# Self attention of a transformer decoder layer on one core: merged narrow blocks, batches of units, and tables that place every maximum singly

## The reference

```python
q, k, v = heads(yn @ wq.T + bq), heads(yn @ wk.T + bk), heads(yn @ wv.T + bv)
scores = einsum('bhqd,bhkd->bhqk', q, k) / sqrt(32) + rel_bias + causal   # 2048 x 2048 for each head
attn = softmax(scores, axis=-1)
y = y + merge(einsum('bhqk,bhkd->bhqd', attn, v)) @ w_out.T + b_out
```

## Time and profile before

| what | value |
|---|---|
| median of 3 runs | 2791.2 us (2790.24 to 2792.56) |
| the profiled execution | 2795.43 us, span 2793.4 us, mean granted clock 0.987 |
| TensorE matmul busy | 2702.4 us, 97% |
| VectorE busy | 1583.1 us, 57% |
| ScalarE busy | 1262.0 us, 45% |
| self attention | 396.8 to 1598.7 us |

### The profile page before, as it was taken

One profiled execution on the slowest core, in us unless ns is written; L12 is line 12 of the kernel. 1 busy time (PEld: TensorE's weight loads), 2 busy tenths in 40 slices (PEclk: granted clock), 3 DMA queues, 4 the chain that ended last, 5 costly groups with the idle time before them and its releaser, 6 DMA issues. The chain is left out here.

```text
span 2793.4 us, 40069 instructions
## 1 busy us (share of the span) xinstructions
PE 2702.4 (97%) x12704; PEld 1791.0 (64%) x12704; DVE 1583.1 (57%) x3827; ACT 1262.0 (45%) x2656; POOL 417.2 (15%) x497
## 2 busy tenths in 40 slices
PE   7999989999999999999999899999999999999998
PEld 6788854444444444444444378767778888888886
DVE  5554367777777777777777377567643222222211
ACT  2322113555555555555555545588833322332231
POOL 5000021000000000000000332188556000000000
PEclk9999988999999999999999999999999999999999
DMA  7656663222222222222222398555431000000000
GB/s 223 214 194 200 197 163 83 69 67 69 69 69 70 70 71 69 61 63 60 56 58 54 90 243 259 197 176 182 149 114 50 16 31 31 30 0 30 31 16 15
DMA packets 138950, 272.96 MB, mean 98 GB/s; under 512 B 24886, under 2 KB 56118, under 8 KB 133499
## 3 DMA queue, kind: packets, MB, share of 16 engines
q1 hardware_dynamic: 133530, 255.14, 31.7%
q0 software_dynamic: 5216, 15.33, 1.8%
HBM read 176.02 MB, written 99.98 MB: 99 GB/s over the span
## 5 line engine op out<-in xcount | busy, mean ns | idle before, releaser
L1302 ACT ACTIVATE sa_pr<-sa_st 128x512 f32<-128x512 f32 (+3 forms) x1280 | 611.0, 532 | 536.8 <-DVE sa_st L1365 293.8
L1268 PE MATMUL sa_ov<-sa_pr,sa_v 128*33 128x512 f32 (+3 forms) x2560 | 535.0, 539 | 0.0
L1349 DVE TENSOR_REDUCE sa_part<-sa_mp 128x1 f32<-128x512 f32 x760 | 408.3, 583 | 115.1 <-PE sa_mp L1247 114.3
L1257 PE MATMUL sa_st<-sa_q,sa_k 97*128 97x512 f32 (+3 forms) x1280 | 441.4, 413 | 17.9 <-ACT sa_pr L1302 13.5
L1257 PEld LDWEIGHTS sa_st<-sa_q,sa_k 97*128 97x128 f32 x1280 | 216.3, 189 | 319.7 <-ACT sa_pr L1302 213.0
L1247 PE MATMUL sa_mp<-sa_k,sa_q 96*128 96x512 f32 (+1 forms) x1256 | 362.0, 382 | 10.3 <-PEq L1229 5.3
L1346 DVE CUSTOM_DVE_ANT_0 sa_mp<-sa_mp,sa_ub 128x512 f32<-128x512 f32 (+1 forms) x496 | 308.4, 665 | 77.0 <-PE sa_mp L1247 72.9
L149 PE MATMUL ff_f<-sa_q,ff_w 128*128 128x512 f32 x1024 | 337.2, 390 | 3.1 <-PEq L2068 3.1
L2063 PE MATMUL ff_o<-ff_w,ca_q 128*128 128x512 f32 x1280 | 330.0, 392 | 3.7 <-DVE ca_q L2114 3.7
L2114 DVE TENSOR_TENSOR ca_q<-ca_v,ca_q 128x512 fp32r<-128x512 f32 x128 | 97.5, 762 | 379.3 <-ACT ca_q L2098 379.3
L1268 PEld LDWEIGHTS sa_ov<-sa_pr,sa_v 128*33 128x33 f32 x2560 | 122.0, 110 | 256.2 <-issue 206.6
(11 more groups left out here) (240 smaller groups left out, 3276.7 us busy)
## 6 DMA issues: line engine op xcount, KB each, us to landing
sa_q<-scratch_q SPq DMA_DIRECT2D x96, 256.0 KB, 7.7
sa_k<-scratch_k SPq DMA_DIRECT2D x96, 256.0 KB, 8.9
scratch_q<-sao_qst SPq DMA_DIRECT2D x32, 512.0 KB, 6.6
ca_q<-scratch_q SPq DMA_DIRECT2D x32, 512.0 KB, 4.6
...
sa_v<-scratch_v SPq DMA_DIRECT2D x16, 528.0 KB, 13.0
scratch_o<-sa_osb SPq DMA_DIRECT2D x128, 66.0 KB
```

The lines of the kernel that those rows point to most:

```text
L1257: pe.matmul(st[bank(u, h)][:, 0:w], ks[n.par][:, h, kb * P:(kb + 1) * P], qs[n.par][:, h, g * GW + c0:(g + 1) * GW], start=True, stop=True ...
L1268: last = pe.matmul(ov[64 * h:64 * h + VW, c0:GW], vs[n.par][:, kb, h, :], pr[:, u % 4, h, 0:GW - c0], start=(u in opens), stop=(u in ends))
L1302: act.activation(pr[:, u % 4, h, 0:w], st[bank(u, h)][:, 0:w], ACT.Exp, scale=SCALE).then_inc(s["exp"], 1)
L1349: dve.tensor_reduce(to, tile, AX_X, ALU.max).then_inc(s["red"], 1)
```

## The change

- **Blocks.** A unit may now hold two narrow blocks. Letters name the kinds: F a far block, B the one before the diagonal, D the first diagonal block (512 wide), P the blocks of 384 and 128 columns side by side in one tile for each head, J the block of 256 columns with both heads in one tile. A slot has 36 units and 68 tiles in place of 40 and 80. A tile has one wait for its bank, one exponential, and one bias addition if it has a bias.
- **Batches.** Rounds of two units become batches of two, the last of each group of three: 16 a slot. In batch j TensorE issues the tiles of batch j + 1 with maxima between them, then the values of batch j.
- **Maxima.** Products for one head are placed singly: `MAX_BEFORE[j][i]` says how many go ahead of the i-th tile, the last entry how many follow. A second table, `REDUCED_BEFORE`, gives the order on VectorE. Four single PSUM banks take the place of two double ones. Work for the next slot begins at batch 6, and the turn of group 2 (product 54 of 84) falls into the last batch of the slot before, that of group 3 (83) into batch 5.
- **Opening.** Seven products go before the first score tile, and the first slot has tables of its own.
- **SyncE.** In every slot but the first the queue is now `load(n + 1)`, `row(n, 2)`, `store(n, 0)`, `row(n, 3)`, `row(n + 1, 0)`, `row(n + 1, 1)`, `store(n, 1)`, `store(n, 2)`, `store(n, 3)`. Ahead of the first slot only `row(0, 1)` stands. The table `sa_tb` has 128 more columns, by a DMA of its own.
- **Rooms.** `sa_pr` has six slots for units in place of four; sums and inverses lie in an existing tile.

```diff
-SELF_ORDER = ((0, 2, 3, 1),
-              (2, 4, 1, 6, 0, 3, 7, 5),
-              (6, 10, 3, 7, 4, 11, 1, 8, 0, 9, 2, 5),
-              (5, 12, 15, 0, 1, 3, 2, 13, 8, 14, 10, 11, 7, 9, 6, 4))
-STEPS_FROM = 12
-STEPS_PER_UNIT = (2, 2, 1, 0, 2, 0, 1, 0, 2, 1, 1, 1, 2, 0, 2, 1, 1, 0, 2, 1,
-                  1, 2, 1, 1, 2, 1, 2, 0, 1, 1, 1, 2, 1, 0, 1, 1, 1, 2, 0, 1)
-INVERSE_AT = 4
-OPENING_STEPS = 16
-OPENING_PER_UNIT = (3,) * 8 + (2, 2, 0, 0)
+SELF_ORDER = ('DPJ', 'FPFDFBJ', 'FPFFBJFFFFD', 'FPFFFFJDFBFFFFF')
+BATCHES = ((3,), (2, 2, 3), (2, 2, 2, 2, 3), (2, 2, 2, 2, 2, 2, 3))
+SLOTS = 6
+MAX_FROM = 6
+OPENING_MAX = 32
+MAX_BEFORE = ((1, 2, 0, 1, 0), (2, 3, 0, 0, 1), (1, 1, 3, 0, 0, 1), (4, 0, 1, 1, 0), (0, 1, 3, 0, 0), (0, 0, 1, 0),
+              (2, 2, 0, 1, 3), (0, 1, 0, 1, 1, 2, 4), (1, 2, 0, 1, 1), (1, 1, 0, 1, 3), (3, 0, 1, 3, 1),
+              (0, 1, 3, 0), (0, 0, 2, 0, 0), (2, 0, 2, 1, 0), (0, 0, 2, 1, 1, 1, 0), (0, 0, 1, 3, 1, 0))
+REDUCED_BEFORE = ((4, 0, 0), (6, 0, 0), (3, 3, 0, 0), (3, 1, 2), (4,), (1, 0, 0, 0), (8,), (5, 2, 2), (4, 0, 1),
+                  (6,), (8,), (2, 0, 0, 2), (1, 1, 0), (5,), (5,), (0, 0, 1, 2, 0, 2))
+OPENING_MAX_BEFORE = ((2, 5, 0, 2, 1), (5, 0, 2, 0, 0), (3, 1, 0, 2, 3, 0), (3, 2, 0, 0, 4), (3, 1, 0, 2, 1),
+                      (2, 2, 0, 2), (0, 2, 0, 0, 5), (2, 1, 2, 0, 1, 0, 0), (1, 1, 1, 3, 1), (0, 2, 2, 0, 1),
+                      (1, 2, 0, 2, 1), (0, 1, 3, 0), (2, 1, 2, 0, 1), (0, 4, 1, 0, 1), (2, 3, 0, 1, 1, 1, 0),
+                      (0, 0, 3, 0, 1, 2))
+OPENING_REDUCED_BEFORE = ((8, 2, 0), (6, 1, 0), (8, 0, 1, 0), (6, 0, 3), (7,), (3, 1, 0, 2), (7,), (6, 0, 0),
+                          (5, 0, 2), (5,), (6,), (0, 3, 0, 1), (5, 1, 0), (6,), (8,), (0, 0, 2, 0, 0, 4))
+INVERSE_AT = 1
+
+
+Unit = namedtuple("Unit", "group tiles")
+Tile = namedtuple("Tile", "parts biased table")
+Part = namedtuple("Part", "head block first at")
...
+def self_max_at(counts, start, NX):
+
+    out, x = [[] for _ in counts], start[1]
+    for j in itertools.chain(range(start[0], len(counts)), range(start[0])):
+        for count in counts[j]:
+            out[j].append([divmod(x + i, NX) for i in range(count)])
+            x += count
+        if j + 1 == len(counts):
+            x -= NX if start[0] else 0
+    return out
...
+        d = TT * g
+        far = iter(range(d - 1))
+        for kind in order:
+            if kind == "F":
+                tiles = both(0, 0, (next(far), 0, 0))
+            elif kind == "B":
+                tiles = both(P, 2 * P, (d - 1, 0, 0))
+            elif kind == "D":
+                tiles = both(2 * P, P, (d, 0, 0))
+            elif kind == "E":
+                tiles = both(2 * P, P, (d + 1, P, 0))
+            elif kind == "K":
+                tiles = both(2 * P, P, (d + 2, 2 * P, 0))
+            elif kind == "L":
+                tiles = both(P, P, (d + 3, 3 * P, 0))
+            elif kind == "P":
+                tiles = both(3 * P, 0, (d + 3, 3 * P, 0), (d + 1, P, P))
             else:
-                out.append((g, kb, 0, P if i == -1 else 0, P))
+                tiles = [Tile([Part(h, d + 2, 2 * P, 2 * P * h) for h in range(2)], 2 * P, P)]
+            out.append(Unit(g, tiles))
+        assert next(far, None) is None and sum(BATCHES[g]) == len(order)
+    return out
+
+
+def self_batches():
...
+    def following(n, j, left):
+
+        if j + 1 < NJ:
+            return [(n, i) for u in batches[j + 1] for i in tiles_of[u]]
+        return [(n + 1, i) for u in batches[0] for i in tiles_of[u]] if left else []
+
+    def places(n, left, places_of, ahead):
+
+
+        for i, places_here in enumerate(places_of):
+            yield [(n + d if d else n, x) for d, x in places_here if left >= d], ahead[i:i + 1]
+
...
-        sums = k.sb(f"{name}_sums", [P, H * T // P])
-        inv = k.sb(f"{name}_inv", [P, H * T // P])
+        sums, inv = (early[5][:, H * T // P * i:H * T // P * (i + 1)] for i in range(2))
...
-        tb = [k.sb(f"{name}_tb{i}", [P, 2, 2 * P]) for i in range(2)]
+        tb = [k.sb(f"{name}_tb{i}", [P, 2, 3 * P]) for i in range(2)]
-        pr = k.sb(f"{name}_pr", [P, 4, 2, GW])
+        pr = k.sb(f"{name}_pr", [P, SLOTS, 2, GW])
-        mp = [k.ps(f"{name}_mp{i}", [P, 2, GW]) for i in range(2)]
+        mp = [k.ps(f"{name}_mp{i}", [P, GW]) for i in range(NMB)]
...
-                sp.dma_start(tb[to][:], dr["sa_T"].ap()[heads].rearrange("h p j -> p h j")).then_inc(s[f"tb{to}"], 16)
+                sp.dma_start(tb[to][:, :, P:3 * P], dr["sa_T"].ap()[heads].rearrange("h p j -> p h j")).then_inc(s[f"tb{to}"], 16)
+                sp.dma_start(tb[to][:, :, 0:P], dr["sa_T"].ap()[heads, :, 0:P].rearrange("h p j -> p h j")).then_inc(s[f"tb{to}"], 16)
...
-                sp.wait_ge(s["red"], 2 * NM * n + 2 * turns[g] + 3)
+                sp.wait_ge(s["red"], NX * n + turns[g] + 2)
...
             load(Step(0, 0, UNROLL), ahead=True)
             sp.wait_ge(s["row"], 32)
             sp.sem_inc(s["row0"], 32)
-            for g in range(1, 3):
-                row(Step(0, 0, UNROLL), g)
+            row(Step(0, 0, UNROLL), 1)
...
             def slot(n, left):
-                if left >= 1:
-                    load(n + 1)
+                if left == 0:
+                    load_sums()
+                if is_first(n):
+                    if left >= 1:
+                        load(n + 1)
+                    store(n, 0)
+                    if left == 0:
+                        store_inverses()
+                    row(n, 2)
+                    row(n, 3)
+                    if left >= 1:
+                        row(n + 1, 0)
+                    store(n, 1)
+                    if left == 0:
+                        load_second()
+                    if left >= 1:
+                        row(n + 1, 1)
+                    store(n, 2)
+                    store(n, 3)
                 else:
-                    load_sums()
-                store(n, 0)
-                if left == 0:
-                    store_inverses()
-                row(n, 3)
-                store(n, 1)
-                if left == 0:
-                    load_second()
-                if left >= 1:
-                    row(n + 1, 0)
-                    row(n + 1, 1)
-                store(n, 2)
-                if left >= 1:
-                    row(n + 1, 2)
-                store(n, 3)
+                    if left >= 1:
+                        load(n + 1)
+                    row(n, 2)
+                    store(n, 0)
+                    if left == 0:
+                        store_inverses()
+                    row(n, 3)
+                    if left >= 1:
+                        row(n + 1, 0)
+                    if left >= 1:
+                        row(n + 1, 1)
+                    store(n, 1)
+                    if left == 0:
+                        load_second()
+                    store(n, 2)
+                    store(n, 3)
             run(sp, N, slot, UNROLL)
...
+            def scores(n, i):
+                u, tile = tiles[i]
+                g = units[u].group
                 if u in opens:
                     pe.wait_ge(s[f"row{g}"], 32 * n + 32)
-                w = GW - c0
-                for h in range(2):
-                    waits(pe, s["exp"], 2 * NU * n + emptied(u, h) + 2)
-                    pe.matmul(st[bank(u, h)][:, 0:w], ks[n.par][:, h, kb * P:(kb + 1) * P],
-                              qs[n.par][:, h, g * GW + c0:(g + 1) * GW], start=True, stop=True).then_inc(s["scores"], 1)
+                waits(pe, s["exp"], NTL * n + emptied(i) + 2)
+                for h, kb, c0, at in tile.parts:
+                    last = pe.matmul(st[i % NST][:, at:at + GW - c0], ks[n.par][:, h, kb * P:(kb + 1) * P],
+                                     qs[n.par][:, h, g * GW + c0:(g + 1) * GW], start=True, stop=True)
+                last.then_inc(s["scores"], 1)
...
-                    values(n, u + 1)
+                    for maxima, ahead in places(n, left, (opening if is_first(n) else usual)[j], following(n, j, left)):
+                        for m, x in maxima:
+                            max_product(m, x)
+                        for m, i in ahead:
+                            scores(m, i)
+                    for u in batches[j]:
+                        values(n, u)
             run(pe, N, slot, UNROLL)
...
+                    biased = [(m, i) for m, i in following(n, j, left) if i in near]
+                    for maxima, ahead in places(n, left, (opening_reduced if is_first(n) else usual_reduced)[j], biased):
+                        for m, x in maxima:
+                            reduce(m, x)
+                        for m, i in ahead:
+                            bias(m, i)
+                    if left == 0 and j == INVERSE_AT:
```

(16 more changed lines are left out.)

249 lines of the change are left out of this document (104 added, 145 removed).

## The result

The changed kernel takes 2865.66 us (median of 4 runs, 2861.57 to 2867.45) against 2791.17 us (4 runs), a ratio of 1.0261 (95%: 1.0245 to 1.0277). It is 74.5 us slower, where 98 were forecast; the profiled execution's span grew from 2793.4 to 2865.5 us, by 72.1.

What follows compares the result with a forecast made beforehand. TensorE was taken as the bound, with 20% of it empty. The terms -59 + 140 + 35 - 18 gave +98 us, so 2889 us as a median, in a range of 2820 to 2945.

Steps and rivals of the forecast that it cites:

- part 1: 14 alike slots: merged blocks, batches and single placing save 4.2 us a slot on TensorE, -59 us (0 to -105).
- part 2: SyncE's queue: group 2's row behind the next loads stalls TensorE 10.0 us in each of 14 slots, +140 us.
- part 3: TensorE's granted clock drops to half behind each stall, 2.5 us a slot, +35 us (0 to +70).
- part 4: First slot's opening rounds: spreading the maxima over all batches wins back half of 34 us lost, -18 us (-8 to -26).
- last slot: Final slot of self attention: fewer rounds traded for batches of six tiles in a row, costed at 0.
- The need: TensorE wants group 2's row, for its first score tile in batch 3, 14.3 us after the slot's first score product.
- The landing: Group 2's row, queued behind `sa_v`, lets TensorE go on 24.3 us after the slot's first score product.
- the row is not held up: Rival on SyncE's queue: the small row passes the loads, landing 15 us into the slot; 2724 us, chance 0.12.
- partial pass: Rival on the DMA engines: the row lands up to 2 us before the last of `sa_v`; 2861 us, chance 0.15.
- the interleaving gives nothing: Rival on TensorE's slots: the 15 us gap stays and part 1 is 0; 2937 us, chance 0.13.
- longer clock: Rival: TensorE's clock stays low 10 us and more a slot, +5 in place of 2.5; 2924 us, chance 0.08.

Runs made afterwards that it cites:

- experiment 1: Changed kernel with group 2's row issued in the slot before, ahead of the last store and the next loads: 2702.73 us, ratio 0.9687.
- Experiment 4: Changed kernel with 36 extra 512-column score products ahead of TensorE's wait for group 2's row in slots 1 to 15: 2836.89 us, ratio 1.0167.
- experiment 2: Kernel before with only group 2's row moved, to right behind the next slot's loads in slots 1 to 15: 2895.61 us, ratio 1.0373.
- Experiment 8: experiment 1 with 12 maxima products in each of the first four batches of slot 0, the rest over the others: 2717.36 us, ratio 0.9748.
- experiment 7: experiment 1 with the alike slots' maxima placed in lots between pairs of tiles instead of singly: 2750.43 us, ratio 0.9858.

## Why the prediction was right, and where its sizes were off

The forecast was 2889 us, slower, in a range of 2820 to 2945; 2865.66 came. The cause is the one it named: one gap a slot in front of the first tile of group 2, ended by the row's DMA, behind it a granted clock of 0.50; experiment 1 takes both away by one moved line. By its terms, in us, measured as experiment 1's slots, the waits, and what remains of the slots' difference:

| term | forecast | measured |
|---|---|---|
| part 1, 14 slots | -59 | -67 (14 x 4.8) |
| part 2, the wait | +140 | +123 |
| part 3, the clock | +35 | +40 (80.24 - 68.61 - 8.77 = 2.86 a slot) |
| part 4, up to the end of slot 0 | -18 | -18.4 |
| last slot, and all behind it | 0 | -5.6 |
| sum (spans) | +98 | +72 |

**Part 2 was the mis-sized term,** 123 us where 140 were reckoned. The need was right: 14.3 us into the slot by the columns of three batches, 14.2 in the mean and 14.1 in the slot shown. The landing was reckoned at 24.3 and came at 23.0 in the mean, by two steps. The loads begin 1.6 us into the slot, not 2.3 (1.7 in the slot shown, 889.07 - 887.41). And the row does not wait for the last of `sa_v`: from the first load to the landing of `sa_v` it takes 21.7 us, as reckoned (21.8), but TensorE goes on 0.3 us before that and not 0.2 after. That gives 23.0 - 14.2 = 8.8 us, the mean wait. (The prediction counts 14 DMAs in a load; they are 15, which changes no term, as it read the times off the rows.)

**Part 1** was put at 3.0 us for the waits and 1.2 for the changes between scores and values. It gave 4.8. Single placing is worth 3.3 of them against placing in two lots, and batches without merged tiles, with the tables tried, are a loss of 3. The 3.0 was a choice between nothing and a bound of 7.5, without a row that gives it, so that the sum came out near is in good part luck. As the prediction took from the Trainium skill (Trainium Kernel Development and Optimization, Performance Expectations), the busy row of TensorE was no guide: in experiment 1's 14 slots it is 958.0 of 960.5 us, though 58.4 of a slot's 68.6 us are columns.

**Part 3** held in size. Experiment 4 shows it as the clock, 2.6 to 2.9 us a slot, and not as some other cost behind the wait. That it is so steady holds for this kernel: in experiment 2 a shorter wait lost more.

**Part 4** held in the sum: 15.7 us in slot 0 and 2.7 before it; what the 2.7 come from is not tested. Experiment 8 shows that the spread of the maxima is worth 15. Two readings behind the 18 were off and did little: in the kernel before four rounds carry 12 maxima, not five (by `OPENING_PER_UNIT` the fifth has 8), and the new table begins with 10, 7, 9, 9, 7, not 8. Half of the 34 us was a choice, not read from a row.

**The last slot**, costed at nothing, is 4.4 us shorter, about what part 1 gives in each other slot. That is the obvious reading; no run tests it.

**The rivals.** That the row is not held up (2724 us) fell by the trace. The partial pass gave 2861 us, nearer to the result than the forecast. It is in part right: the row was there before the last of `sa_v` in 8 of 14 slots, by 1.8 us in the slot shown, so DMAs of one queue did not always complete in the order of their issue. But the mean is 0.3 us and not 2, so against the forecast, which had 0.2 us after it, the pass gives 14 x 0.5 = 7 of the 28 us, and the rest of its nearness is luck. That the interleaving gives nothing fell by experiments 1 and 7. The longer clock, 5 us and more, did not come in this kernel (2.5 to 2.9 us); in some slots of experiment 2 it did.

**What would have mended it.** Experiment 1 is faster than both kernels: 2702.73 us, 3.1% below the kernel before and 163 us below the changed one.
